# Local attention with a transposed product of values, and experts that start inside the attention stage before them

## The chip, the cores and the metric

The kernel runs on one core of one Trainium2 chip, in one launch. The metric is the time of an execution in microseconds (us). The core has four compute engines that run their own instruction streams side by side: TensorE (PE: matrix products and transposes), VectorE (DVE), ScalarE (ACT) and GpSimd (POOL). SyncE (SP) issues DMAs. Engines meet only through semaphores. PE writes into PSUM, which has eight banks, each of 512 fp32 numbers for each of 128 partitions; the other data lie in SBUF.

## The reference

A residual stream x of 2048 rows of 128 numbers goes through eight blocks, each `x = x + block(...)`:

```
linear attention
FFN block: 2 layers of local attention and gated FFN
small attention, global and local
FFN block again
head attention: softmax over the 16 heads of a row
experts
full attention: blocks of 256 rows, 2 heads
experts
```

The change touches four of them. The **FFN block** works on 2 x 1024 rows, so on 16 tiles of 128 rows, twice (2 layers). Cut to what matters, one layer is

```
h = shift_token(x)                 # half of the channels come from the row before
q, k, v = split(h @ wqkv)          # 8 heads of 64
q, k = rotary(l2norm(q) * qs, l2norm(k) * ks)
sim = q @ k^T  over windows of 64 rows and the window before, masked
x = x + (softmax(sim) @ v) @ wo
h = layernorm(shift_token(x)) @ w1 + b1
x = x + (a * gelu(g)) @ w2 + b2    # a, g = the halves of h, 341 wide
```

The **experts** are

```
logits = x @ Ws.T + bs;  probs = softmax(logits)     # 8 experts
route = argmax(probs);   xf = x * max(probs)
perm = argsort(route)                                # rows sorted by expert
y = relu(xf[perm] @ W1[e] + b1[e]) @ W2[e] + b2[e]
out = row i of the result is y of the i-th routed row (in sorted order)
```

The sorted rows go back into the stream in their sorted places, so each row's place has to be known before its result can be sent.

## The kernel before, in words

Eight stages stand in one program: linear attention, `windows(0)`, `small_heads`, `windows(1)`, `head_attention`, `experts(0)`, `full_attention`, `experts(1)`. After each stage every engine drains and adds to `batch_done`; SP waits for all four, sets the semaphores back to zero (`clear`) and lets them go on through `batch_go`.

Nothing plans the order. Each engine has its own loop over steps t, and the order of calls in that loop's body is the order of its instructions.

**`windows(F)`** runs 32 tiles (16 tiles, 2 layers) as a pipeline. In step t PE computes the scores of tile t (L522: 32 products in two banks), projects q and k of tile t + 2 (L531, L534), turns q and k of tile t + 1 (`turn_qk`, L550 and L557), turns the normalised output of tile t - 2 (`turn_out`, L593), turns the probabilities of tile t - 1 (`turn_probs`, L568), multiplies the output of tile t - 2 by wo (`out_rows`, L600), multiplies the probabilities of tile t - 1 by v (`values`, L582) and projects v of tile t + 2 (L541). Four tiles make a group for the FFN: its products (L625 up, L637 down) and its transposes (L328) stand in fixed steps. A cycle of four steps therefore repeats eight times in a pass and sixteen times in the program. Its steps are called A (down, first gates), B (last gate, L328), C (first two values of the FFN, `g_hm`) and D (last value, L328 of the FFN's input). A step begins with L522.

DVE takes the masked scores with their row minima (L1677), rotates q and k (L1684, L1685), sums the squares (L1706, L1707), adds the attention's output to the rows (`add_out`, L1700), multiplies the FFN's halves (`mid`, L1721), takes the reciprocal of the softmax sums (L1712) and scales the product of values with it (`norm_out`, L1668). Statistics of a group's shifted rows are L1456 and L1463. ACT squares q and k (L1103, L1105), copies banks to SBUF (L980), takes the exponentials (L1136) and the gelu (L1171, L1172). POOL adds the halves of the rotated pairs (`turn_pairs`, L2222, L2225), takes a power for the norms of q and k (L2232, L2235) and multiplies k with its own (L2233). SP copies the rows before a window (`lookback`) and the shifted rows of the FFN's input (`shift`, L2414 and L2415), in this order in each step.

**`head_attention`** has 16 tiles. For each, POOL multiplies 2048 columns of probabilities by values (`mix`, L2279) and DVE forms and adds up products of the same size (L1836, L1863).

**`experts(k)`** has a front for each of four chunks of 512 rows: variance (L1971, L1974), centring (L1982), normalisation on ACT, transposes, logits, shift (L1987 and the two after it), softmax and argmax (`route`, L1996 to L2005), scaled transposes, ranks on PE, prefix sums (L2012, L2013). POOL fetches each row's bias with an indirect DMA of one row per partition (L2319, 16 of them). Then 32 units follow, one for each pair of chunk and expert: PE up (L903), ACT relu, PE down (L911), DVE adds the rows that belong to the expert (L2034). After unit 8 DVE computes all rows' places (L2019 to L2023, `e_idx`), and POOL sends the 16 tiles of finished rows, with an indirect DMA each (L2329). A send needs its places and its chunk's last unit. The sorted rows are read back by SP (L2397). The first unit waits for the four biases of chunk 0.

## Time and profile before

| | us |
|---|---|
| median of 3 runs | 1928.71 (1919.35 to 1932.64) |
| the profiled execution | 1929.18 |
| its span in the profile | 1927.4 |
| PE busy in the span | 1617.2 (84%) |
| DVE busy | 1223.1 (63%) |
| ACT busy | 1071.9 (56%) |
| POOL busy | 906.4 (47%) |
| mean granted clock of TensorE | 0.916 of full speed |

The stages show in the trace as follows, by the first and last instructions of each: linear attention to about 328 us, `windows(0)` to about 720, `small_heads` to about 1058, `windows(1)` to about 1450, head attention from 1451 to 1599, the first experts to 1699, full attention to 1827, the second experts to the end. A row of a timeline gives start and length in us, engine, line, operation, the buffers written and read, how many instructions were joined to one row, and in brackets how long the engine had been idle before and what ended it. The busy shares are means over stages with different limits, so a wait counts only in the stage in which it ends last.

### The profile page before, as it was taken

The numbers are of one execution on the slowest core, as the hardware profiler recorded it, in microseconds if no ns is written. First come the engines' busy times: TensorE is split into PE (matmuls) and PEld (weight loads), VectorE is DVE, ScalarE is ACT, GpSimd is POOL, SyncE is SP. The second block draws the span as 40 slices with busy tenths as digits, with TensorE's granted clock in tenths as the row PEclk, the third lists the DMA queues.
The fourth block names the chain that finished last, engine by engine and source line by source line (L and its number), as shares of the span: only waits on it lengthen the run. The fifth ranks groups of instructions, "written<-read, shape, count | busy, mean of one in ns | idle before, by whom it ended". The sixth has DMA issues, their size and how long they took to land.

```text
span 1927.4 us, 37986 instructions
## 1 busy us (share of the span) xinstructions
PE 1617.2 (84%) x13323; PEld 1156.0 (60%) x13323; DVE 1223.1 (63%) x3746; ACT 1071.9 (56%) x2753; POOL 906.4 (47%) x668
## 2 busy tenths in 40 slices
PE   5999997799999977899787799999976666958777
PEld 5999995566666643344454466666644544636555
DVE  3555554887777644555763787777746985636565
ACT  3655653788888834566542678888842113323332
POOL 1333333776667512223443777667614673422044
PEclk9999998999999987899776999999987896968989
DMA  5000000111111100000000111111100001210012
GB/s 208 1 2 1 1 2 6 26 34 26 33 27 29 25 5 1 1 1 2 1 2 1 25 32 27 29 31 27 33 6 0 1 1 39 23 28 1 15 30 23
DMA packets 41082, 38.64 MB, mean 20 GB/s; under 512 B 21944, under 2 KB 32192, under 8 KB 40512
## 3 DMA queue, kind: packets, MB, share of 16 engines
q1 hardware_dynamic: 35264, 32.02, 6.4%
q0 software_dynamic: 5632, 4.20, 1.8%
q8 instruction: 110, 1.80, 0.4%
q14 instruction: 76, 0.62, 0.1%
HBM read 13.14 MB, written 4.20 MB: 9 GB/s over the span
## 4 chain that ended last, share of the span: by engine, by line
PE 46%; DVE 15%; issue 11%; POOL 7%; ACT 4%; DMA 1%; POOLq 0%; DVEq 0%; SPq 0%; ACTq 0%
PE ps L687 4%; PE ps L625 3%; PE ps L522 3%; PE ps L531 3%; PE ps L328 3%; PE ps L568 3%; PE ps L582 2%; PE ps L534 2%; PE ps L600 2%; PE ps L903 2%; PE ps L637 2%; PE ps L700 2%; PE ps L541 2%; PE ps L911 2%; POOL arena L2279 1%
## 5 line engine op out<-in xcount | busy, mean ns | idle before, releaser
L980 ACT ACTIVATE arena<-ps 128x512 f32<-128x512 f32 (+4 forms) x670 | 356.8, 589 | 273.8 <-PE ps L328 100.1
L1219 ACT ACTIVATE arena<-ps 128x320 f32<-128x320 f32 (+4 forms) x256 | 132.5, 561 | 136.5 <-PE ps L687 133.6
L1136 ACT ACTIVATE arena<-arena,g_small 128x128 f32<-128x128 f32 x512 | 198.7, 406 | 0.5
L2182 POOL TENSOR_TENSOR arena<-arena,consts 128x512 f32<-128x512 f32 (+1 forms) x64 | 93.1, 1455 | 195.3 <-ACT arena L1219 195.2
L1677 DVE CUSTOM_DVE_ANT_0 arena<-ps,consts,g_ss 128x128 f32<-128x128 f32 x512 | 145.6, 347 | 58.7 <-PE ps L522 58.7
L2222 POOL TENSOR_TENSOR arena<-arena 128x512 f32<-128x512 f32 x64 | 81.9, 1279 | 176.8 <-DVE arena L1685 176.8
L687 PE MATMUL ps<-arena 32*128 32x160 f32 (+4 forms) x1024 | 123.0, 471 | 22.6 <-ACT arena L1219 10.2
L328 PE MATMUL ps<-consts,arena 128*128 128x128 f32 x400 | 80.9, 339 | 59.1 <-ACT arena L1332 11.8
L1684 DVE TENSOR_TENSOR arena<-ps,tabs 128x512 f32<-128x512 f32 x128 | 87.7, 686 | 52.7 <-ACT arena L1105 46.0
L687 PEld LDWEIGHTS ps<-arena 32*128 32x128 f32 x1024 | 62.1, 214 | 91.1 <-ACT arena L1219 54.1
L328 PEld LDWEIGHTS ps<-consts,arena 128*128 128x128 f32 x400 | 55.6, 172 | 98.0 <-DVE arena L1475 20.6
L2232 POOL TENSOR_TENSOR g_ss<-g_ss,consts 128x8 f32<-128x8 f32 x64 | 105.4, 1647 | 9.7 <-DVE g_ss L1707 3.7
L1559 DVE TENSOR_REDUCE arena<-arena 128x8 f32<-128x1032 f32 x32 | 39.3, 1228 | 109.3 <-ACT arena L1037 109.3
L2279 POOL TENSOR_TENSOR arena<-arena 128x2048 f32<-128x2048 f32 x16 | 86.9, 5442 | 44.6 <-ACT arena L1241 44.6
L625 PE MATMUL ps<-arena,weights 128*128 128x512 f32 (+1 forms) x192 | 96.0, 610 | 13.6 <-ACT arena L1165 5.6
L2153 POOL TENSOR_TENSOR arena<-arena,consts 128x8 f32<-128x8 f32 x32 | 52.7, 1648 | 113.6 <-DVE arena L1559 113.6
L1136 ACT ACTIVATION_READ_ACCUMULATOR arena<-arena,g_small 128x1 f32 x512 | 105.1, 205 | 0.0
L2235 POOL TENSOR_TENSOR g_ss<-g_ss,consts 128x8 f32<-128x8 f32 x64 | 104.8, 1638 | 0.0
L749 PE MATMUL ps<-arena,consts 128*128 128x256 f32 x256 | 72.4, 446 | 34.5 <-DVE arena L1836 34.5
L2034 DVE SCALAR_TENSOR_TENSOR arena<-ps,arena 128x128 f32<-128x128 f32 x256 | 72.0, 344 | 42.8 <-PE ps L911 30.3
L700 PE MATMUL ps<-arena 128*32 128x160 f32 (+4 forms) x1024 | 88.7, 420 | 5.0 <-issue 5.0
L522 PEld LDWEIGHTS ps<-arena 64*64 64x64 f32 x2048 | 57.6, 135 | 58.4 <-issue 58.4
(257 smaller groups left out, 4170.3 us busy)
## 6 DMA issues: line engine op xcount, KB each, us to landing
arena<-arena SPq DMA_DIRECT2D x112, 128.0 KB, 2.3
weights<-in_w SPq DMA_DIRECT2D x1, 5069.0 KB, 24.2
weights<-in_w SPq DMA_DIRECT2D x1, 2052.0 KB, 12.6
arena<-Y SPq DMA_DIRECT2D x64, 32.0 KB
arena<-Y SPq DMA_DIRECT2D x64, 31.8 KB
consts<-in_c SPq DMA_DIRECT2D x1, 1278.0 KB, 8.7
sorted_rows<-X SPq DMA_DIRECT2D x1, 1024.0 KB, 5.1
X<-sorted_rows SPq DMA_DIRECT2D x4, 256.0 KB, 3.5
```

What stands on the lines that cost most here:

```text
L328: last = tr(ps[:, bank, j * P:(j + 1) * P], src(j), ident)
L522: last = mm(ps[64 * r:64 * r + 64, 4 + hf, i * P:(i + 1) * P], g_qT[rows, i, 64 * r:64 * r + 64], g_kT[rows, i, at:at + P], start=True, st ...
L625: mm(ps[0:m, 4 + c % 2, :], W("f_w1", at, at + m), g_hnT, start=True, stop=True)\
L687: last = mm(ps[:, 2 * (st % 2) + hh, 0:n], b_kT[rows, k % 2, r, j * P:(j + 1) * P], b_qT[rows, k % 2, j * P:j * P + n], start=True, stop=True)
L700: last = mm(ps[rows, 6 + U % 2, j * P:j * P + n], b_vx[:, k % 2, j, g, :], b_p[:, U % 2, g, at:at + n], start=j == 0, stop=True, skip_grou ...
L980: copy = lambda o, i: act.activation(o, i, ACT.Copy)
L1136: last = act.activation(g_p[:, n % 2, 4 * hf + i, :], g_sc[:, 4 * hf + i, :], ACT.Exp, scale=-1.0, bias=g_mn[:, h:h + 1], accum_out=g_rs[: ...
L1219: act.activation(b_p[:, U % 2, 2 * gp:2 * gp + 2, at:at + n], ps[:, b:b + 2, 0:n], ACT.Exp, scale=float(HD) ** -0.5).then_inc(s.b_exp, 1)
L1677: last = dve.tensor_tensor_reduce(g_sc[:, 4 * hf + i, :], ps[:, 4 + hf, i * P:(i + 1) * P], C("mask_f" if n % NT else "mask_f0"), g_ss[:, ...
L2232: stepped_after(pool.tensor_tensor(ss[:, 8:16], ss[:, 8:16], C("neghalf", 0, 8), ALU.pow))
L2235: pool.tensor_tensor(ss[:, 0:8], ss[:, 0:8], C("neghalf", 0, 8), ALU.pow).then_inc(gs.root, 1)
L2279: pool.tensor_tensor(c_mix[:, u % 2].rearrange("p (h d t) -> p h d t", h=HB, t=HB), c_e[:, u % 2].unsqueeze(2).broadcast_to(full), vals.un ...
```

## The change

It has two parts.

In **`windows`** the product of values swaps its operands: v becomes the stationary side and the turned probabilities the moving one, so that the output comes out with heads and channels on partitions, as `out_rows` needs it. The number and size of the products stay. `turn_out` and `norm_out` are gone. Since a row's reciprocal can no longer be applied after the product, the probabilities are scaled ahead of `turn_probs`: the even heads by DVE (`scale_even`, at the end of the tile's own step), the odd ones by POOL (`scale_odd`, first in the step after). `turn_probs` waits for the scaled halves. ACT copies the output from bank 3 as the first thing of a step (`keep_out`), and `out_rows` moves ahead of `turn_probs`. On DVE the statistics of the FFN's input move one step earlier (from `at_step` 7 to 6), behind the minima; `add_out` goes between the rotations, the FFN's multiplications ahead of the sums of squares.

In the **experts** the drain, `clear` and `batch_go` ahead of both expert stages are gone. Their SBUF area moves behind that of the attention. The front of chunk 0, and the variances of the first chunks, stand in the last steps of the attention stage; those of chunks 1 to 3 stand at units 0, 7 and 14 and the six after each. DVE computes all places after unit 19. The first unit no longer adds to fetched biases, so it doesn't wait for their DMA; POOL adds them later. In the first experts the last tile's sums and the last addition of head attention stand between the units 3 and 7.

```diff
+        front_bank, up_banks, down_banks = (4, 7), ((0, 1), (5, 6)), ((2, 3), (0, 1))
+        turned_at = (None, 0, 7, 14)
...
-                    pe.wait_ge(gs.exp, 2 * N + hf + 1)
+                    pe.wait_ge(gs.odd if hf else gs.even, N + 1)
...
-                    need(pe, gs.os, N)
+                    need(pe, gs.oin, N)
                     need(pe, gs.hin, m0 + groups_by(t, -3))
                     need(pe, gs.y, m0 + groups_by(t, 12))
-                    for h in range(HF):
+                    for i in range(4):
                         for r in range(2):
-                            src = g_v if r else g_vx
-                            last = mm(ps[64 * r:64 * r + 64, 3, h * DF:(h + 1) * DF],
-                                      g_pT[:, 4 * (h % 2) + h // 2, 64 * r:64 * r + 64],
-                                      src[:, j, h * DF:(h + 1) * DF], start=True, stop=True, skip_group_check=True)
+                            for hf in range(2):
+                                h, src = 2 * i + hf, g_v if r else g_vx
+                                last = mm(ps[64 * hf:64 * hf + 64, 3, i * P + 64 * r:i * P + 64 * r + 64],
+                                          src[:, j, h * DF:(h + 1) * DF], g_pT[:, 4 * hf + i, 64 * r:64 * r + 64],
+                                          start=True, stop=True, skip_group_check=True)
                     last.then_inc(gs.pv, 1)
-
-                def turn_out(n):
-                    N = n0 + n
-                    pe.wait_ge(gs.os, N + 1)
-                    pe.wait_ge(gs.vin, n0 + tiles_by(n + 3))
-                    need(pe, gs.add, N)
-                    for c in range(4):
-                        last = tr(ps[:, 2, c * P:(c + 1) * P], g_os[:, c * P:(c + 1) * P], ident)
-                    last.then_inc(gs.ot, 1)
 
                 def out_rows(n):
                     N, l = n0 + n, n // 16
                     pe.wait_ge(gs.oin, N + 1)
+                    pe.wait_ge(gs.vin, n0 + tiles_by(n + 3))
+                    need(pe, gs.add, N)
                     for c in range(4):
                         last = mm(ps[:, 2, 0:D], g_oT[:, c, :], W("f_wo", 512 * l + 128 * c, 512 * l + 128 * c + 128),
                                   start=c == 0, stop=c == 3)
                     last.then_inc(gs.out, 1)
...
-                        turn_out(t - 2)
+                        out_rows(t - 2)
...
                 def keep_out(n):
                     N = n0 + n
-                    act.wait_ge(gs.ot, N + 1)
+                    act.wait_ge(gs.pv, N + 1)
                     need(act, gs.out, N)
-                    copy(g_oT, ps[:, 2, :].rearrange("p (c t) -> p c t", c=4)).then_inc(gs.oin, 1)
+                    copy(g_oT, ps[:, 3, :].rearrange("p (c t) -> p c t", c=4)).then_inc(gs.oin, 1)
...
+                    if live(t - 2):
+                        keep_out(t - 2)
                     if live(t + 2):
                         squares(t + 2)
                     if live(t + 1):
                         keep_qk(t + 1)
-                    if live(t - 2):
-                        keep_out(t - 2)
...
-
-                def norm_out(n):
+                halves = lambda t: t.rearrange("p (i f) -> p f i", f=2)
+
+                def reciprocals(n, hf):
                     N = n0 + n
-                    dve.wait_ge(gs.pv, N + 1)
-                    need(dve, gs.ot, N)
-                    tt(heads(g_os), heads(ps[:, 3, :]), wide(g_ri, [P, HF, DF], 2), ALU.mult).then_inc(gs.os, 1)
+                    ri, rs = halves(g_ri)[:, hf, :], halves(g_rs[:, n % 2, :])[:, hf, :]
+                    dve.wait_ge(gs.exp, 2 * N + hf + 1)
+                    if hf:
+                        need(dve, gs.odd, N)
+                        dve.reciprocal(ri, rs).then_inc(gs.odd_ri, 1)
+                    else:
+                        need(dve, gs.even, N)
+                        after(dve.reciprocal(ri, rs), True)
+
+                def scale_even(n):
+                    probs = g_p[:, n % 2, 0:4, :]
+                    tt(probs, probs, wide(halves(g_ri)[:, 0, :], [P, 4, P], 2), ALU.mult).then_inc(gs.even, 1)
...
-                    if at_step(t, 7):
+                    if live(t):
+                        minima(t, 0)
+                    if live(t - 1):
+                        reciprocals(t - 1, 1)
+                    if fresh:
+                        norm_var(0)
+                    if live(t):
+                        minima(t, 1)
+                    if at_step(t, 6):
                         dve.wait_ge(gs.sh, 176 * (m0 + group + 1))
                         norm_stats(1, g_h)
-                    if live(t):
-                        minima(t, 0)
-                    if fresh:
-                        norm_var(0)
-                    if at_step(t, 7):
                         norm_var(1)
-                    if live(t):
-                        minima(t, 1)
                     if live(t + 2):
                         rope_k(t + 2)
+                    if live(t - 2):
+                        add_out(t - 2)
                     if fresh:
                         norm_apply(0, y, x, gs.ln)
                     if live(t + 2):
                         rope_q(t + 2)
-                    if live(t - 2) and at_step(t, 10):
-                        add_out(t - 2)
-                    if live(t + 2):
-                        sums(t + 2)
-                    if live(t - 2) and not at_step(t, 10) and not at_step(t, 12):
-                        add_out(t - 2)
+                    for lag, half, c in FFN_STEPS:
+                        if half == 1 and at_step(t, lag):
+                            mid((t - lag) // 4, c)
                     if at_step(t, 7):
                         need(dve, gs.hnt, m0 + group)
                         norm_apply(1, g_hn, g_h, gs.h2)
-                    if live(t - 1):
-                        reciprocals(t - 1)
+                    if live(t + 2):
+                        sums(t + 2)
+                    if live(t):
+                        reciprocals(t, 0)
+                        scale_even(t)
                     if at_step(t, 12):
                         add_down((t - 12) // 4)
-                    if live(t - 2) and at_step(t, 12) and not at_step(t, 10):
-                        add_out(t - 2)
-                    for lag, half, c in FFN_STEPS:
-                        if half == 1 and at_step(t, lag):
-                            mid((t - lag) // 4, c)
-                    if live(t - 1):
-                        dve.wait_ge(gs.dve_step, stepped.n)
-                        norm_out(t - 1)
...
+                    if t == 12:
+                        shift_routed(0, 0)
...
+                    if t == 13:
+                        route(0, 0)
+                    if t == 15:
+                        prefix(0, 0)
                     z, r = (t + 6) // NT, (t + 6) % NT
                     if z < NB and r == 0:
...
-                        prefix(q // 3 + 1)
-                    if q == 8:
-                        places_of_all()
+                    if k == 0 and q == 3:
+                        values(TT - 1)
+                        centre(0, 2)
+                    if k == 0 and q == 7:
+                        add_rows(NB - 1)
+                        variance(0, 3)
+                    if q == (9 if k == 0 else 1):
+                        centre(k, 3)
+                    for c in range(1, NB):
+                        if q == turned_at[c]:
+                            shift_routed(k, c)
+                        elif q == turned_at[c] + 1:
+                            route(k, c)
+                        elif q == turned_at[c] + 5:
+                            prefix(k, c)
+                    if q == turned_at[3] + 5:
+                        places_of_all(k)
...
+                def scale_odd(n):
+                    probs = g_p[:, n % 2, 4:8, :]
+                    ri = g_ri.rearrange("p (i f) -> p f i", f=2)[:, 1, :]
+                    pool.wait_ge(gs.odd_ri, n0 + n + 1)
+                    pool.tensor_tensor(probs, probs, ri.unsqueeze(2).broadcast_to([P, 4, P]), ALU.mult)\
+                        .then_inc(gs.odd, 1)
...
                 for t in range(-4, TILES + 9):
+                    if live(t - 1):
+                        scale_odd(t - 1)
...
+                fetch_biases(0)
+                fetch_biases(1)
+                if k == 0:
+                    root_routed(0, 3)
+                fetch_biases(2)
+                pool.wait_ge(b2_sem[0], 16 * NT * (k + 1))
+                pool.wait_ge(es.e_acc_in, (E * NB - 1) * k + E)
+                pool.tensor_tensor(e_acc[:, 0:NT, :], e_acc[:, 0:NT, :], e_bias, ALU.add).then_inc(es.e_bias_in, 1)
+                fetch_biases(3)
                 pool.wait_ge(es.e_idx_in, k + 1)
                 pool.wait_ge(es.e_kept, 16 * (k + 1))
+                pool.wait_ge(es.e_bias_in, k + 1)
...
-                sp.wait_ge(batch_done, 4)
-                clear()
-            if STAGES >= 6:
+                sp.wait_ge(s.c_add, NB)
                 keep(scratch.rearrange("(i p) d -> p i d", p=P))
                 back()
-            if STAGES >= 7:
                 sp.wait_ge(batch_done, 1)
                 clear()
```

Three places show what moves. First PE in step C of `windows`; before:

```order
L522 MATMUL ps<-arena 64x128 x16
L531 MATMUL ps<-weights,arena 128x512
L534 MATMUL ps<-weights,arena 128x512
L550 MATMUL ps<-consts,arena 128x128 x4
L557 MATMUL ps<-consts,arena 128x128 x4
L593 MATMUL ps<-consts,arena 128x128 x4
L625 MATMUL ps<-arena,weights 128x512 x2
L568 MATMUL ps<-consts,arena 128x128 x8
L600 MATMUL ps<-weights,arena 128x128 x4
L582 MATMUL ps<-arena 64x64 x16
```

and with the change (L527 is L522, L599 is `out_rows`, L624 up, L573 `turn_probs`, L588 `values`):

```order
L527 MATMUL ps<-arena 64x128 x16
L536 MATMUL ps<-weights,arena 128x512
L539 MATMUL ps<-weights,arena 128x512
L555 MATMUL ps<-consts,arena 128x128 x4
L562 MATMUL ps<-consts,arena 128x128 x4
L599 MATMUL ps<-weights,arena 128x128 x4
L624 MATMUL ps<-arena,weights 128x512 x2
L573 MATMUL ps<-consts,arena 128x128 x8
L588 MATMUL ps<-arena 64x64 x16
```

The four transposes are gone, and `out_rows` no longer stands between `turn_probs` and `values`. Next DVE in the same step, behind the minima; before:

```order
L1684 TENSOR_TENSOR arena<-ps,tabs 128x512
L1685 TENSOR_TENSOR arena<-ps,tabs 128x512
L1684 TENSOR_TENSOR arena<-ps,tabs 128x512
L1685 TENSOR_TENSOR arena<-ps,tabs 128x512
L1700 TENSOR_TENSOR Y<-Y,ps 128x128
L1706 TENSOR_REDUCE g_ss<-arena 128x16
L1707 TENSOR_SCALAR g_ss<-g_ss 128x16
L1712 RECIPROCAL g_small<-g_small 128x8
L1721 SCALAR_TENSOR_TENSOR arena<-ps,weights,arena 128x512 x2
L1668 TENSOR_TENSOR arena<-ps,g_small 128x512
L1456 BN_STATS stats<-arena 128x6 x4
```

and with the change (L1476 to L1489 are the statistics, L1736 and L1737 the sums, L1694 the reciprocals, behind which `scale_even` follows):

```order
L1476 BN_STATS stats<-arena 128x6 x4
L1483 BN_AGGR mv<-stats 128x2 x4
L1489 TENSOR_SCALAR g_rstd<-mv 128x4
L1714 TENSOR_TENSOR arena<-ps,tabs 128x512
L1715 TENSOR_TENSOR arena<-ps,tabs 128x512
L1730 TENSOR_TENSOR Y<-Y,ps 128x128
L1714 TENSOR_TENSOR arena<-ps,tabs 128x512
L1715 TENSOR_TENSOR arena<-ps,tabs 128x512
L1745 SCALAR_TENSOR_TENSOR arena<-ps,weights,arena 128x512 x2
L1736 TENSOR_REDUCE g_ss<-arena 128x16
L1737 TENSOR_SCALAR g_ss<-g_ss 128x16
L1694 RECIPROCAL g_small<-g_small 128x4
```

The statistics, which wait for SP's shifted rows, and the FFN's multiplications now stand ahead of the sums. Last, DVE in the first experts with the change, around the places (L2085 is the unit's addition, four to a unit; L2067 writes `e_idx`):

```order
L2085 SCALAR_TENSOR_TENSOR arena<-ps,arena 128x128 x16
L2056 TENSOR_TENSOR arena<-arena,ps 128x8 x4
L2057 TENSOR_TENSOR arena<-ps,arena 128x32
L2063 TENSOR_TENSOR arena<-arena 128x1 x7
L2064 TENSOR_TENSOR arena<-arena 128x128
L2065 TENSOR_TENSOR arena<-arena 128x128
L2066 TENSOR_REDUCE arena<-arena 128x16
L2067 CAST e_idx<-arena 128x16
L2085 SCALAR_TENSOR_TENSOR arena<-ps,arena 128x128 x48
```

Behind `e_idx` 48 additions are left, which is 12 units; before there were 92, which is 23.

## Rows read from the trace of the kernel before

**Rows 1.** stretch: bounds, length, busy us per engine, TensorE clock, DMA share, GB/s.
```profile
1067.00:1403.00 336.00, 311.90 (x3252) 217.43 (x3252) 260.67 (x924) 270.71 (x801) 229.70 (x173) 0.98 0.13 29
```

**Rows 2.** timeline of TensorE, local attention: start, us, what, [idle before <-releaser].
```profile
500.41 1.10 PE L522 MATMUL ps<-arena 64*64 64x128 f32 x32 [0.16 <-DVE arena L1721]
...
522.91 1.10 PE L522 MATMUL ps<-arena 64*64 64x128 f32 x32
...
526.63 0.60 PE L593 MATMUL ps<-consts,arena 128*128 128x128 f32 x4
...
530.05 1.13 PE L600 MATMUL ps<-weights,arena 128*128 128x128 f32 x8
...
534.43 1.10 PE L522 MATMUL ps<-arena 64*64 64x128 f32 x32 [1.12 <-DVE arena L1721]
...
544.45 1.10 PE L522 MATMUL ps<-arena 64*64 64x128 f32 x32 [0.16 <-DVE arena L1721]
```

**Rows 3.** timeline of ScalarE, the same step.
```profile
526.94 0.61 ACT L1172 ACTIVATE arena<-arena 85x512 f32<-85x512 f32 x1
...
528.41 2.52 ACT L980 ACTIVATE arena<-ps 128x512 f32<-128x512 f32 x5
```

**Rows 4.** timeline of VectorE, the same step.
```profile
528.55 0.69 DVE L1684 TENSOR_TENSOR arena<-ps,tabs 128x512 f32<-128x512 f32 x1 [2.22 <-ACT arena L1105]
...
531.42 1.21 DVE L1706 TENSOR_REDUCE g_ss<-arena 128x16 f32<-128x1024 f32 x1
...
532.88 1.41 DVE L1721 SCALAR_TENSOR_TENSOR arena<-ps,weights,arena 128x512 f32<-128x512 f32 x2
...
534.80 0.86 DVE L1456 BATCH_NORM_STATS2 stats<-arena 128x6 f32<-128x128 f32 x4
...
536.69 0.38 DVE L1463 BATCH_NORM_AGGREGATE mv<-stats 128x2 f32<-128x6 f32 x4
```

**Rows 5.** timeline of GpSimd, the same step.
```profile
529.92 1.28 POOL L2222 TENSOR_TENSOR arena<-arena 128x512 f32<-128x512 f32 x1 [4.64 <-DVE arena L1685]
...
532.92 1.65 POOL L2232 TENSOR_TENSOR g_ss<-g_ss,consts 128x8 f32<-128x8 f32 x1 [0.37 <-DVE g_ss L1707]
534.65 1.04 POOL L2233 TENSOR_TENSOR arena<-arena,g_ss 128x512 f32<-128x512 f32 x1
```

**Rows 6.** timeline of SyncE's DMA queue, the same step.
```profile
526.58 0.92 SPq L2415 DMA_DIRECT2D arena<-Y  x1
```

**Rows 7.** timeline of VectorE, inside head attention.
```profile
1523.72 2.94 DVE L1883 SCALAR_TENSOR_TENSOR c_nm<-mv,g_rstd 128x4 f32<-128x4 f32 x1
```

**Rows 8.** timeline of GpSimd, the same moment.
```profile
1521.19 5.45 POOL L2279 TENSOR_TENSOR arena<-arena 128x2048 f32<-128x2048 f32 x1 [2.42 <-ACT arena L1241]
```

**Rows 9.** timeline of VectorE, end of head attention, then first experts.
```profile
1591.94 2.29 DVE L1863 TENSOR_REDUCE ps<-arena 128x128 f32<-128x2048 f32 x1 [2.08 <-POOL arena L2279]
...
1608.06 0.19 DVE L1987 TENSOR_TENSOR arena<-ps,rows 128x32 f32<-128x32 f32 x1 [4.03 <-PE ps L883]
...
1610.72 0.69 DVE L2005 TENSOR_TENSOR arena<-arena 128x512 f32<-128x512 f32 x1
...
1626.66 1.12 DVE L2034 SCALAR_TENSOR_TENSOR arena<-ps,arena 128x128 f32<-128x128 f32 x4 [5.78 <-DMA arena<-bias_rows,e_rt]
...
1649.14 0.17 DVE L2023 CAST e_idx<-arena 128x16 uint32<-128x16 f32 x1
...
1684.91 1.13 DVE L2034 SCALAR_TENSOR_TENSOR arena<-ps,arena 128x128 f32<-128x128 f32 x4 [0.62 <-PE ps L911]
```

**Rows 10.** timeline of GpSimd, last of the first experts' sends.
```profile
1694.10 1.56 POOL L2329 DMA_INDIRECT sorted_rows<-arena,e_idx  x1 [0.30 <-issue]
```

**Rows 11.** timeline of SyncE's DMA queue, end of the first experts.
```profile
1697.43 2.02 SPq L2397 DMA_DIRECT2D X<-sorted_rows  x4
```

**Rows 12.** timeline of VectorE, full attention's last rows, second experts' first unit.
```profile
1826.51 0.17 DVE L1932 RECIPROCAL m_rs<-m_rs 128x2 f32<-128x2 f32 x1 [2.16 <-PE ps L845]
...
1854.94 1.13 DVE L2034 SCALAR_TENSOR_TENSOR arena<-ps,arena 128x128 f32<-128x128 f32 x4 [5.83 <-DMA arena<-bias_rows,e_rt]
```

509 lines of the change are left out of this document (260 added, 249 removed).

## The prediction

> **What bounds the kernel now.** I read the stages first. In the second pass of local attention TensorE is busy in 311.9 of 336 us at nearly full clock, while VectorE and ScalarE stay near 80% [rows 1]. So that stage goes by TensorE, and a microsecond taken from TensorE is a microsecond gained, as long as nothing that TensorE waits for comes later. Next comes TensorE's timeline for one cycle [rows 2]. The scores of step A start at 500.41 and those of the next A at 544.45, so four tiles take 44.04; C, from 522.91 to 534.43, takes 11.52 of it. In the whole cycle TensorE waits visibly twice, 1.12 in front of D and 0.16 in front of A, both times for `mid`.
>
> The experts are bound otherwise. The last `mix` ends at 1591.91, where VectorE starts its last sum, and the first unit starts at 1626.66 after a wait for the fetched biases [rows 9]: 34.7 us with no unit. From there to the reading back at 1697.43 [rows 11] it is 70.8. VectorE's units stand 1.75 apart (1.13 busy, 0.62 idle in front, at 1684.91 [rows 9]), and the last four sends 1.86 apart (1.56 busy, 0.30 idle) [rows 10]. In the second experts the gap from the last rows of attention, 1826.51, to the first unit at 1854.94 is 28.4 [rows 12].
>
> **Local attention, what goes.** `turn_out` costs TensorE from 526.63 to the next product at 527.07, 0.44 us for each of 64 tiles: 28.2 us. The wait of 1.12 in front of D goes too, since `mid` now stands ahead of the sums, and the 0.16 in front of A: 1.3 in a cycle. The swapped products keep their count and size, and I cost them at nothing (bounds: 32 records in 1.1 us either way; the width that moves is 64 in both). `norm_out` leaves VectorE; `scale_even` comes, of the same size as a rotation's product at 0.69 [rows 4], so its load hardly changes.
>
> **Local attention, what comes.** Times are counted from the start of C (522.91).
>
> 1. ScalarE's second gelu ends at +4.6, since its table load and two gelus stand ahead of the step [rows 3]. `keep_out` takes 0.5 (five copies in 2.52), so `out_rows` can start at about +5.2. TensorE is ready for it at +3.7, where `turn_out` stood [rows 2]. Before, the copy stood there too, but the up products and `turn_probs` hid it. TensorE waits about 1.4.
> 2. `out_rows` (530.05, 1 us) stood between `turn_probs` and `values` and hid ScalarE's copy of the turned probabilities. In C nothing is left between the two; the copy and its two semaphores cost about 0.8. In A, B and D products of the FFN stand there.
> 3. SP's last shifted rows are issued at +3.7 to +4.6 [rows 6], behind `lookback`, and nothing in the change moves that. With some 1.6 for landing they are there at +6.2. VectorE now waits for them in C; before, it read them in D. Then statistics 0.86 and the two small steps, 1.4 together, four rotations 2.4, `add_out` 0.2, `mid` 1.3, sums 1.4 [rows 4]: the sums end at +12.9. Before they ended at +9.9.
> 4. GpSimd's power takes 1.65 and the product with k 1.04 [rows 5]: k is ready at about +15.6, which is +3.9 in D. TensorE wants it at +3.3, and waits about 0.7.
> 5. The second power, 1.64, and `scale_odd` follow. The nearest row for the latter is the product with k, 1.04, the same size with a broadcast factor; the other bound is `turn_pairs` at 1.28 [rows 5]. I take 1.04. The odd half of `turn_probs` waits about 0.8 in D. The delay is not made up in D, where VectorE has no idle time: A begins with 0.2 and 0.8 of the same two waits.
>
> A cycle: -1.76 - 1.3 + 1.4 + 0.8 + 0.7 + 0.8 + 1.0 = +1.6. Sixteen cycles give +26. At the ends of each pass, where TensorE has no other tiles, the scalings stand in the open: some 2 us a pass, +4. **Local attention: +30.** From +24 (each wait 0.1 less) to +38 (`scale_odd` at 1.28 in every tile on the path).
>
> **First experts.** The first unit no longer waits for a DMA and starts about when the last `mix` ends: -34.7. Put into the attention's last steps are two variances, 2.8 together, and a chunk's shift and route, from 1608.06 to the end of the scaling at 1611.4, 3.4 [rows 9]. Centring is a few hundred numbers, but in head attention such an instruction took 2.94 us: it began at 1523.72 and ended with a `mix` of 5.45 that began at 1521.19 [rows 7, 8]. Two of them: 5.9. Prefix and what route meets of a `mix`: about 2. So the attention is later by 14. The units: before, nine of them with two fronts and the places took 22.6, from 1626.66 to 1649.3. Now `e_idx` needs eleven more units (19.3), one front (3.4) and the last sums, addition and variance of head attention (2.6 + 0.7 + 1.4): 50.0. Then 15 sends at 1.86, 27.9, and from the last one to the reading back 3.3, with 0.4 to the first: 81.6 against 70.8, +10.8. GpSimd is the bound there: the last unit would be done at 50 + 12 x 1.75 = 71. Sum: -34.7 + 14 + 10.8 = **-10**.
>
> **Second experts.** -28.4, and about 6.7 for what is left between the last values and the first unit; three variances and a route in the attention, 7.6 (there is no `mix`); the unit stage is longer as above without head attention's sums, 6.1. **-8**. What the missing drains save lies in these gaps.
>
> **Sum.** 1929.2 + 30 - 18 = 1941.2 for the profiled execution, against a median of 1928.7 that is 0.5 lower. I predict **1941**, slightly slower. About 1%, or 19 us, is what can be told from no change: between 1909 and 1948 is the same.
>
> The Trainium skill ("SBUF — State Buffer", "Who interferes with whom") says that a VectorE instruction with two SBUF inputs and a GpSimd instruction that reads SBUF exclude each other, the later one blocking fully. The 2.94 us above agree. By that rule `scale_even`, whose two inputs lie in SBUF, would wait for `turn_pairs` or the powers, and the sum would be rival 2's.
>
> **Rivals.**
>
> 1. *The waits don't appear, and TensorE keeps its 28 us.* It needs the copy of the output, the sums and `scale_odd` in time. For it: TensorE's 93% [rows 1], and GpSimd idle for 4.64 before `turn_pairs` [rows 5], room for 1.04. Against it: the place behind the gelu and SP's rows, which are orders in the code. Time: 1929.2 - 28 - 18 = 1883. Chance 0.25.
> 2. *VectorE and GpSimd hold each other up in every tile* (slower). `scale_even` starts with GpSimd's power and is held for its 1.65; then the next minima are late, and a chain that had 20% to spare on VectorE loses 0.5 in each of 64 tiles: +32. Time: 1973. It decides if a `scale_even` takes over 1.5 us. For it: [rows 7, 8]. Against it: `mid`, with two inputs in SBUF, took its 0.7 each at 532.88 while the power ran from 532.92 [rows 4, 5]. Chance 0.15.
> 3. *The experts gain the whole gap.* If the parts in the attention fit into VectorE's waits for `mix` (2.08 us in the last step [rows 9]) and the sends are not the bound, each stage gains about 28, together -56: 1929.2 + 30 - 56 = 1903. Against it: sixteen sends after `e_idx`, a count in the code. Chance 0.13.
>
> The forecast has the remaining 0.47, from 1918 to 1962 by its own bounds (24 to 38 for local attention; -30 to -5 for the experts, if the centrings are not held or if route is held twice).
>
> Faster by over 1%: rival 1 nearly whole and half of 3, 0.31. Slower by over 1% (over 1948): rival 2 and a third of the forecast, 0.31. The same: 0.38. The range goes from 1880, which takes in most of rival 1, to 1966; outside are rival 2 and the best ends of 1 and 3 together.
>
> **What would show it.** Right: in step C TensorE waits for ScalarE's copy ahead of `out_rows` and ahead of `values`, VectorE waits for a DMA behind the minima, and in D the transposes of k and of the odd probabilities wait for GpSimd; a cycle of 45.5; `e_idx` at 50 us after the first unit, and 16 sends in a row. Wrong: a cycle of 42 to 43 (rival 1), `scale_even` longer than 1 us (rival 2), or sends that end with the last unit (rival 3).

## The result

| | before | changed |
|---|---|---|
| median | 1927.51 us (1919.35 to 1932.64, 4 runs) | 1961.22 us (1958.54 to 1964.84, 4 runs) |
| profiled execution, its span | 1929.18, 1927.4 | 1962.28, 1960.4 |

The changed kernel is slower by 1.5%: ratio 1.0152, 95% interval 1.0115 to 1.0189. The forecast was 1941 with a range of 1880 to 1966 and 0.31 for slower by over 1%. The time lies in the range; the likeliest case had its sign, and about a third of its size.

The table splits the difference of the two spans, 33.0 us, by stages. Each border is the start or end of an instruction that both traces show.

| stretch | before | changed | difference | forecast |
|---|---|---|---|---|
| to the first statistics of head attention | 1451.1 | 1492.4 | +41.3 | +30 |
| from there to the end of the last `mix` | 140.8 | 155.4 | +14.6 | +14 |
| to the first unit | 34.7 | 0 | -34.7 | -34.7 |
| first unit to the reading back | 70.8 | 84.1 | +13.3 | +10.8 |
| full attention, first statistics to last rows | 126.3 | 137.0 | +10.7 | +7.6 |
| to the first unit | 28.4 | 7.4 | -21.0 | -21.7 |
| first unit to the end | 72.5 | 81.4 | +8.9 | +6 |

(0.1 lies between the reading back and full attention.) The second half of the change gains 8.2 in all; the first loses 41.3. Of these, 35.9 lie between the first and the last scores of the two passes of local attention. Some stages also differ between traces of the same instructions: from the last scores of the first pass to the first of the second it is 403.7 before and 406.4 changed, but 400.4 in the trace of `e_only` and 415.6 in that of `e_centre` below, which have the same code there; the granted clock between 720 and 1058 us was 0.83 and 0.77. A difference of a few microseconds in that stretch or in head attention is therefore no reading of the change.

**Local attention.** TensorE's waits from 350 to 650 us, total, times and longest. Before, the first was the one for `mid`:

```profile
PE ps L522 <- DVE arena L1721: 6.3, 10, 1.1
```

With the change they are:

```profile
PE ps L588 <- ACT arena L996: 13.6, 17, 1.4
PE ps L573 <- POOL arena L2285: 9.8, 13, 1.7
PE ps L599 <- ACT arena L996: 6.6, 5, 1.4
PE ps L562 <- POOL arena L2265: 5.4, 8, 1.3
```

These are `values` (L588) and `out_rows` (L599) behind ScalarE's copies, and the odd half of `turn_probs` (L573) and the transposes of k (L562) behind GpSimd's multiplications. TensorE was busy in 284.1 of these 300 us before and is in 259.4 now. Its timeline, with the same columns and for the same tiles as in [rows 2]; 535.07 begins the step C that began at 522.91 there:

```profile
532.68 1.15 PE L588 MATMUL ps<-arena 128*64 128x64 f32 x32 [0.71 <-ACT arena L996]
...
535.07 1.10 PE L527 MATMUL ps<-arena 64*64 64x128 f32 x32 [0.18 <-issue]
...
540.26 1.16 PE L599 MATMUL ps<-weights,arena 128*128 128x128 f32 x8 [1.30 <-ACT arena L996]
...
542.98 1.04 PE L573 MATMUL ps<-consts,arena 128*128 128x128 f32 x8
544.75 1.15 PE L588 MATMUL ps<-arena 128*64 128x64 f32 x32 [0.74 <-ACT arena L996]
...
547.27 1.10 PE L527 MATMUL ps<-arena 64*64 64x128 f32 x32 [0.32 <-DVE arena L1745]
...
551.37 0.66 PE L562 MATMUL ps<-consts,arena 128*128 128x128 f32 x4 [0.64 <-POOL arena L2265]
...
553.97 0.66 PE L573 MATMUL ps<-consts,arena 128*128 128x128 f32 x4 [0.62 <-POOL arena L2285]
...
558.00 1.10 PE L527 MATMUL ps<-arena 64*64 64x128 f32 x32
```

TensorE waits 1.30 for the copy ahead of `out_rows`, 0.74 ahead of `values`, 0.32 for `mid` at D's start, 0.64 for k and 0.62 for the odd half in D. B, whose end is the first row, waits 0.71 ahead of `values`; that one the forecast didn't have. ScalarE, VectorE, GpSimd in that order, each with the timeline's columns:

```profile
539.12 0.61 ACT L1188 ACTIVATE arena<-arena 85x512 f32<-85x512 f32 x1
539.64 0.57 ACT L996 ACTIVATE arena<-ps 128x512 f32<-128x512 f32 x1
```

```profile
541.73 0.87 DVE L1476 BATCH_NORM_STATS2 stats<-arena 128x6 f32<-128x128 f32 x4 [3.17 <-DMA arena<-Y]
...
547.05 1.21 DVE L1736 TENSOR_REDUCE g_ss<-arena 128x16 f32<-128x1024 f32 x1
...
548.58 0.71 DVE L1698 TENSOR_TENSOR arena<-arena,g_small 128x512 f32<-128x512 f32 x1
```

```profile
548.54 1.65 POOL L2264 TENSOR_TENSOR g_ss<-g_ss,consts 128x8 f32<-128x8 f32 x1 [1.32 <-DVE g_ss L1737]
550.27 1.05 POOL L2265 TENSOR_TENSOR arena<-arena,g_ss 128x512 f32<-128x512 f32 x1
551.27 1.64 POOL L2267 TENSOR_TENSOR g_ss<-g_ss,consts 128x8 f32<-128x8 f32 x1
552.87 1.05 POOL L2285 TENSOR_TENSOR arena<-arena,g_small 128x512 f32<-128x512 f32 x1
```

`keep_out` stands behind the gelu at +4.6 (539.64), as [rows 3] let expect. VectorE waits 3.17 for SP's rows and begins the statistics at +6.7, half a microsecond later than taken: SP issued the last of them at +3.7 to +4.6 as forecast, and they came 2.05 behind that, not 1.6; the sums (with L1737 behind the row shown) end at +13.4, not at +9.9 as in [rows 4]. GpSimd's k is there at 551.3, `scale_odd` (L2285) ends at 553.9, and TensorE's two rows in D start 0.05 to 0.06 behind each. `scale_odd` took 1.05 and `scale_even` (548.58) 0.71: both as taken.

The steps of the settled part of a pass (tiles 12 to 28 of its 32), start of the scores to start of the scores, for the kernel before and those that differ from it in local attention:

```
                 A      B      C      D     cycle
before         12.71   9.79  11.53  10.02   44.05
changed        13.32  10.06  12.20  10.73   46.31
w_only         13.32  10.06  12.20  10.72   46.30
w_no_odd       12.49  10.05  12.21  10.07   44.82
w_ko           13.32  10.05  12.20  10.72   46.29
w_ko_stats7    13.33  10.05  10.62  11.34   45.34
w_v_first      13.12  10.06  12.20  10.71   46.09
w_best         11.93  10.06  11.70  10.99   44.68
b_one_turn     12.72   9.78  11.52  10.02   44.04
b_eight_turns  13.00  10.09  11.53  10.03   44.65
```

**Experts.** VectorE at the end of head attention and in the first units, and GpSimd's sends with the `mix` that ran beside the first row:

```profile
1582.00 2.78 DVE L2023 SCALAR_TENSOR_TENSOR arena<-arena 128x4 f32<-128x4 f32 x1
...
1617.04 2.53 DVE L2039 TENSOR_TENSOR arena<-arena 128x32 f32<-128x32 f32 x1
...
1647.68 1.11 DVE L2082 TENSOR_SCALAR arena<-ps,arena 128x128 f32<-128x128 f32 x4
...
1699.78 0.17 DVE L2067 CAST e_idx<-arena 128x16 uint32<-128x16 f32 x1
```

```profile
1579.35 5.42 POOL L2320 TENSOR_TENSOR arena<-arena 128x2048 f32<-128x2048 f32 x1 [2.42 <-ACT arena L1257]
...
1700.23 1.63 POOL L2375 DMA_INDIRECT sorted_rows<-arena,e_idx  x1 [4.78 <-DVE e_idx L2067]
...
1728.37 1.57 POOL L2375 DMA_INDIRECT sorted_rows<-arena,e_idx  x1 [0.31 <-issue]
```

The centring of chunk 0 (L2023) took 2.78 and ended at 1584.78, as the `mix` did (1584.77): the instruction was held, as [rows 7, 8] showed of its like. That of chunk 1 fell between two `mix` and took 0.15. A product of `route` (L2039) was held for 2.53. The first unit (L2082) starts 0.05 before the last `mix` ends, in place of 34.7 behind it [rows 9]. `e_idx` comes 52.1 behind the first unit, and then the sixteen sends stand in a row to 1728.37, the reading back following at 1731.78.

In full attention the last rows begin at 1871.67 and the first unit at 1879.05, where [rows 12] had 28.4 between the two:

```profile
1871.67 0.17 DVE L1968 RECIPROCAL m_rs<-m_rs 128x2 f32<-128x2 f32 x1 [2.16 <-PE ps L856]
...
1879.05 1.13 DVE L2082 TENSOR_SCALAR arena<-ps,arena 128x128 f32<-128x128 f32 x4 [3.88 <-PE ps L938]
```

The stage is longer by 10.7 where 7.6 was forecast. TensorE's queue shows one reason: the scaled transposes of chunk 0 stand ahead of the last products of attention and wait for VectorE's `route`:

```profile
1861.54 1.12 PE L333 MATMUL ps<-consts,arena 128*128 128x128 f32 x4 [3.18 <-DVE arena L2046]
```

### The profile page after: what moved, and what is told of

Read it like the earlier page. It is cut to its first block and busy times, and to the rows that moved or that the text cites. A ratio compares the mean times of both kernels' runs of the same rounds, so it can differ in the third digit from the quotient of the medians.

```text
span 1960.4 us, 37569 instructions
## 1 busy us (share of the span) xinstructions
PE 1597.3 (81%) x13067; PEld 1126.3 (57%) x13067; DVE 1242.6 (63%) x3810; ACT 1078.4 (55%) x2753; POOL 978.9 (50%) x734
## 5 line engine op out<-in xcount | busy, mean ns | idle before, releaser
L996 ACT ACTIVATE arena<-ps 128x512 f32<-128x512 f32 (+4 forms) x670 | 371.0, 578 | 345.5 <-PE ps L333 92.8
L333 PE MATMUL ps<-consts,arena 128*128 128x128 f32 x400 | 76.5, 325 | 44.5 <-DVE arena L1672 10.5
L624 PE MATMUL ps<-arena,weights 128*128 128x512 f32 (+1 forms) x192 | 98.7, 624 | 14.0 <-ACT arena L1181 7.5
L746 PE MATMUL ps<-arena,consts 128*128 128x256 f32 x256 | 77.1, 468 | 34.8 <-DVE arena L1855 34.8
L588 PEld LDWEIGHTS ps<-arena 128*64 128x64 f32 x2048 | 65.6, 138 | 65.9 <-ACT arena L996 33.3
L588 PE MATMUL ps<-arena 128*64 128x64 f32 x2048 | 74.1, 225 | 29.0 <-ACT arena L996 29.0
L1152 ACT ACTIVATION_READ_ACCUMULATOR arena<-arena,g_small 128x1 f32 x512 | 97.4, 190 | 0.0
L599 PE MATMUL ps<-weights,arena 128*128 128x128 f32 x512 | 72.8, 287 | 27.9 <-ACT arena L996 27.9
```

Of the source, the lines that this page charges most:

```text
L333: last = tr(ps[:, bank, j * P:(j + 1) * P], src(j), ident)
L588: last = mm(ps[64 * hf:64 * hf + 64, 3, i * P + 64 * r:i * P + 64 * r + 64], src[:, j, h * DF:(h + 1) * DF], g_pT[:, 4 * hf + i, 64 * r:64 ...
L624: mm(ps[0:m, 4 + c % 2, :], W("f_w1", at, at + m), g_hnT, start=True, stop=True)\
L996: copy = lambda o, i: act.activation(o, i, ACT.Copy)
L1152: last = act.activation(g_p[:, n % 2, 4 * hf + i, :], g_sc[:, 4 * hf + i, :], ACT.Exp, scale=-1.0, bias=g_mn[:, h:h + 1], accum_out=g_rs[: ...
```

## The experiments

**The two halves apart.** `w_only` is the kernel before with the change in `windows` and nothing else, `e_only` the reverse; the edit is the diff ahead of the prediction, cut in two.

> The kernel before with the change in local attention alone; head attention and experts are as before. My theory (the two parts add up, and local attention carries the loss): head attention starts 41 us later in the trace of the changed kernel, and everything behind it is as before, so 1928 + 41 = 1969, with the same cycle of 46.3. The rival (part of those 41 us comes from the other half of the change, by its memory layout or its code) expects under 1960.

> The kernel before with the change in the experts alone. My theory, from the two traces: the first experts gain 34.7, lose 14.6 in the attention before them and 13.3 in their units and sends; the second gain 21.0 and lose 10.7 and 8.9; together -8, so 1920. The rival (the missing drains are worth more, and the late start of both stages in the changed kernel hides it) expects 1900 or less.

Measured: w_only 1973.8 us, ratio to before 1.0217 (1.0169 to 1.0265); e_only 1918.5, ratio 0.9966 (0.9934 to 0.9997). The rivals fall: local attention alone loses some 42 us with the same steps, and the experts alone gain 0.3%, 6.5 us by that ratio (12.5 by the medians), with the 8 expected inside the interval. Within these intervals the halves add up.

**GpSimd's multiplication left out.**

```diff
-                    pool.tensor_tensor(probs, probs, ri.unsqueeze(2).broadcast_to([P, 4, P]), ALU.mult)\
-                        .then_inc(gs.odd, 1)
+                    pool.sem_inc(gs.odd, 1)
```

> As w_only, without GpSimd's multiplication of the odd heads' probabilities: they stay unscaled, the semaphore is raised all the same. My theory (GpSimd's chain of powers, product with k and this product ends TensorE's waits in A and D, and part of B): the waits of turn_probs go, the ones for k go partly, the cycle falls from 46.3 by 1.3 to 1.6, that is 21 to 26 us less than w_only. Rival 1 (VectorE's late sums set the pace, GpSimd's product only stands in their shadow): under 8 us less. Rival 2 (the shared SBUF port): over 35 less, since the products of both engines no longer meet.

Measured: 1945.1 us, ratio 1.008 (1.0033 to 1.0126), 29 less than w_only. The cycle fell by 1.48, inside the expected 1.3 to 1.6; A lost 0.83 and D 0.65. Rival 1 is out (under 8), and so is rival 2 (over 35). One multiplication of 1.04 us in each tile costs 24 us in the sixteen cycles, 0.37 a tile, though GpSimd was idle for a quarter of this stage (busy 226.6 of 300 us in w_only): in two of the four steps it stands last in a chain, in the other two (10.05 and 12.20 with it, 10.05 and 12.21 without) it costs nothing.

**Which waits are worth what.** Four kernels change the order of w_only.

```diff
 # w_ko, ScalarE's loop
-                    if live(t - 2):
-                        keep_out(t - 2)
...
+                    if live(t - 1):
+                        keep_out(t - 1)
                     if at_step(t, 9):
                         gelu((t - 9) // 4)
 # w_ko_stats7, besides: VectorE
+                    if at_step(t, 7):
+                        dve.wait_ge(gs.sh, 176 * (m0 + group + 1))
+                        norm_stats(1, g_h)
                     if live(t):
                         minima(t, 0)
 # w_v_first, on w_only, TensorE
-                    if live(t - 1):
-                        values(t - 1, t)
                     if live(t + 2):
                         project_v(t + 2, t)
+                    if live(t - 1):
+                        values(t - 1, t)
```

`w_best` is w_ko_stats7 with w_v_first's order and the sums ahead of `mid`.

> As w_only, with two orders changed: ScalarE copies the output of a tile at the end of the step, ahead of the gelu, instead of behind it at the start of the next; and VectorE's statistics of the shifted rows go back to step D, ahead of the minima. My theory (the place behind the gelu and the wait for SP's rows are two of the four losses): TensorE's 1.3 in C ahead of out_rows and VectorE's 3.2 are gone, the waits for GpSimd in D shrink; the cycle falls to between 44.5 and 45.2, that is 18 to 29 us less than w_only. The rival (one wait takes the other's place) expects within 6 us of w_only.

> As w_only, with ScalarE's copy of the output at the end of a step, ahead of the gelu; the statistics stay in step C, behind the wait for SP's rows. Theory 1 (the waits add up): the 1.3 us ahead of out_rows in C are saved in each cycle, 20 us less than w_only. Theory 2 (the chain from SP's rows through VectorE's sums and GpSimd sets when k of step D is ready, so TensorE reaches D earlier and waits there): C falls by 1.3 or more, D grows by nearly as much, at most 6 us less than w_only. I hold theory 2 for likelier, 0.7.

> As w_only, with the projection of v for tile t + 2 ahead of the product of values of tile t - 1 on TensorE, so that 1 us of work stands where TensorE waited for ScalarE's copy of the turned probabilities. Theory 1 (that wait is lost time in B and C): 0.7 in each of two steps, cycle 46.3 to 44.9, 22 us less than w_only. Theory 2 (in C the chain from SP's rows sets the end of the step, only B can gain): cycle to 45.6, 8 to 12 us less. Theory 3 (B's gain too is only waited for later, at GpSimd's half of turn_probs): under 4 us less. I hold theory 2 for likeliest.

> As w_ko_stats7, with the sums of squares ahead of the FFN's multiplications on VectorE, as before the change, and the projection of v ahead of values on TensorE: every order that was found to cost is undone or filled, and the four transposes stay away. Theory 1 (the transposes filled a gap in which TensorE would have waited for ScalarE's copies of q and k, so leaving them out saves nothing, and GpSimd's multiplication of the odd heads still costs): cycle 44.2 to 45.0, 1935 to 1945, no faster than before. Theory 2 (TensorE's 28 us come out once the new waits are gone): cycle under 43.2, 1915 or less.

Measured, as ratios to before: w_ko_stats7 1.0113 (1.0057 to 1.0168), w_ko 1.0178 (1.0148 to 1.0208), w_v_first 1.022 (1.0182 to 1.0258), w_best 1.0035 (1.0008 to 1.0062), its median 1937.0.

In w_ko the wait of 1.3 is gone and no step is shorter. TensorE's table shows it again in front of D, for `mid` (L1716), up to 1.5:

```profile
PE ps L521 <- DVE arena L1716: 7.4, 5, 1.5
```

So theory 2 holds: C ends when the chain from SP's rows ends. Only with the statistics back in D does C fall, by 1.58, and D gives back 0.62; A stays. The cycle was 45.34, just outside the expected 44.5 to 45.2. In w_v_first the waits of `values` fell from w_only's 13.6 to 1.1 in the same 300 us, and the cycle by 0.2: theory 3, the one held for least likely. In its place TensorE waits at a step's start for ScalarE's copy of a gate (L1156), and the rows for GpSimd stay:

```profile
PE ps L567 <- POOL arena L2243: 10.7, 15, 1.7
...
PE ps L521 <- ACT arena L1156: 5.6, 5, 1.2
...
PE ps L582 <- ACT arena L971: 1.1, 2, 0.6
```

w_best came out as its theory 1 had it, 44.68 and 1937: without the four transposes, a cycle is still longer than with them. But the steps differ. A, in which TensorE has no idle row, is 0.78 shorter than before. The others end with longer waits: 1.16 ahead of C for the copy of a gate, 1.83 and 1.45 ahead of D and A for `mid`. In the same 300 us, where before it was 6.3 for `mid` and none for the gate, these are:

```profile
PE ps L521 <- DVE arena L1716: 16.4, 10, 1.8
...
PE ps L521 <- ACT arena L1156: 5.6, 5, 1.2
```

TensorE was busy in 261.6 of the 300 us, against 284.1 before. So its work is gone, and outside A the time was waited away. w_best still has `scale_odd`, and `mid` behind the sums. No run left `scale_odd` out of it or of w_ko_stats7, so what the new order of TensorE is worth without GpSimd in the chain is open.

**What the transposes were worth.** In the kernel before, three of a tile's four transposes are left out (b_one_turn), or all are done twice (b_eight_turns).

```diff
-                    for c in range(4):
+                    for c in range(1):                      # b_one_turn
+                    for c in (0, 1, 2, 3, 0, 1, 2, 3):      # b_eight_turns
                         last = tr(ps[:, 2, c * P:(c + 1) * P], g_os[:, c * P:(c + 1) * P], ident)
```

> The kernel before, with one transpose of a tile's output in place of four (the other three quarters of the output are left out), everything else the same. It asks what the removed TensorE work was worth by itself. Three transposes are 0.33 us in each of 64 tiles, 21 us. My theory (the stage goes by TensorE): 15 to 21 us less than before; the 1.3 us a cycle that TensorE waits for mid may take up to 6 of it back. The rival (TensorE's work was never the bound, the chain through GpSimd was) expects under 6 us.

> The kernel before, with a tile's four transposes of the output done twice, 0.43 us more of TensorE in each of 64 tiles, the same result. With three of four left out, the cycle of 44.04 stayed. Theory 1 (the four transposes just fill the gap in which turn_probs waits for ScalarE's copies of q and k, so work beyond them counts): A and B grow by 0.4 each, C and D by less, as they waited 1.1 and 0.2 for mid; cycle 45.0 to 45.8, 15 to 28 us slower. Theory 2 (the gap is wider, or TensorE is not what sets the step): cycle under 44.3, under 4 us slower.

b_one_turn: 1927.3 us, ratio 0.9978 (0.9951 to 1.0006), no step changed by over 0.01. The lower end of the interval alone would leave 9 us, the steps leave none. My theory falls. TensorE's timeline of its step A:

```profile
502.19 1.10 PE L522 MATMUL ps<-arena 64*64 64x128 f32 x32 [0.16 <-DVE arena L1721]
...
505.92 0.27 PE L593 MATMUL ps<-consts,arena 128*128 128x128 f32 x1
506.43 1.12 PE L568 MATMUL ps<-consts,arena 128*128 128x128 f32 x8 [0.24 <-issue]
```

In A the scores start at 502.19 and `turn_probs` at 506.43, 4.24 later, as before (500.41 and 504.65); the transpose is shorter, and an idle time of 0.24 stands behind it. From 350 to 650 us such idle times are 7.8 in 27 tiles, against 0.3 in one tile before, and the wait for `mid` is 6.3 in both:

```profile
PE ps L568 <- issue: 7.8, 27, 0.6
```

27 times the 0.33 that was left out is 8.9: nearly all of it came back as waiting. The profile names no releaser for it. By the code the first half of `turn_probs` waits for ScalarE's copy of the turned q, whose bank it overwrites. ScalarE's timeline of the kernel before has that copy as the first of the five behind the squares of k:

```profile
503.46 0.60 ACT L1105 ACTIVATE arena<-ps 128x512 f32<-128x512 f32 x1 [0.26 <-PE ps L534]
503.95 2.55 ACT L980 ACTIVATE arena<-ps 128x512 f32<-128x512 f32 x5
```

and in b_one_turn

```profile
505.74 2.55 ACT L980 ACTIVATE arena<-ps 128x512 f32<-128x512 f32 x5
```

`turn_probs` starts 0.70 and 0.69 behind these, and in C of the kernel before 0.69 behind 528.41 [rows 3]. Taken singly, the copy lasts 0.59 and `turn_probs` starts 0.10 behind its end in each step between 450 and 590 us of both kernels, whatever TensorE did just before. In b_eight_turns, where the transposes reach further, it starts in A, B and D 0.46 behind the copy and 0.11 behind the start of the last transpose, the usual distance between two transposes. So `turn_out` was work put into a gap. No run moved the copy; that it ends the gap is read from the code and from this constant distance, while the worth of the transposes in that order is measured. b_eight_turns: 1939.5, ratio 1.007 (1.0038 to 1.0101), cycle 44.65, between the ranges of both theories. A and B grew by 0.3 each, C and D by nothing, though each of them got 0.43 more. The gap in A and B ends about 0.1 behind the four transposes; in C and D TensorE has at least 0.43 to spare.

**The experts.** `e_early` brings the fronts closer, `e_centre` moves the centrings, `e_early_centre` does both and moves the variances as well.

```diff
-        turned_at = (None, 0, 7, 14)     # fronts; scaled transposes at + 5, ranks at + 6
+        turned_at = (None, 0, 5, 11)     # e_early; + 3 and + 4
 # e_centre, VectorE in head attention
                     if 0 <= t - 1 < TT:
                         shift(t - 1)
+                    if t in (9, 13):
+                        centre(0, t // NT - 2)
...
                     if t in (8, 12):
                         variance(0, t // NT - 2)
-                    if t in (9, 13):
-                        centre(0, t // NT - 2)
```

> As e_only, with the fronts of chunks 1 to 3 closer together: they begin at units 0, 5 and 11 instead of 0, 7 and 14, and a chunk's scaled transposes and ranks follow 3 and 4 units behind its start instead of 5 and 6. All places are then known after unit 14 instead of 19. Theory 1 (the sixteen sends behind the places bound the stage): from the first unit to the reading back it falls from 84 us to 79, where the last unit and its four sends (10.8) take over; 5 us in each stage, 1909. Theory 2 (TensorE and VectorE pace the units, the sends keep pace): nothing, 1918.

> As e_early, with the variances and centrings of chunks 0 and 1 ahead of the sum over the mixed values in head attention's steps, where GpSimd's mix of 5.4 us does not run, instead of at the end of the step, where it does. In the changed kernel they took 1.71, 2.78 and 1.06 there in place of 0.17. Theory (these small instructions are held by the shared read port until the mix ends, and VectorE's products wait behind them): each takes under 0.3, and head attention is 4 to 5 us shorter; 1905. The rival (mix is the bound, VectorE has the time): the instructions are short but the stage ends as before.

> As e_only, with the two centrings of head attention alone moved ahead of the sum over the mixed values; the variances stay at the step's end. Theory (a small instruction of VectorE with two SBUF inputs is held until GpSimd's mix ends): the centring of chunk 0 takes 0.15 in place of 2.91, and head attention from its first statistics to the end of the last mix falls by 2 to 3 us from 159.2; 1916 in place of 1918.5. The rival (VectorE has that time to spare) expects the same length.

e_early: ratio 0.9953 (0.9935 to 0.9971), median 1919.5. `e_idx` came 47.4 behind the first unit in place of 50.4, but the stage took 83.5 in place of 82.3 in e_only: twelve sends ran in a row, and then GpSimd waited for the last units:

```profile
1682.32 1.56 POOL L2376 DMA_INDIRECT sorted_rows<-arena,e_idx  x1 [4.49 <-DVE arena L2095]
```

Theory 2 is right: sends and units were nearly level, and the fronts put closer together slow the units.

e_early_centre: ratio 0.9977 (0.9957 to 0.9998). The centrings took 0.15 as expected. The variances' last instruction, one addition to 4 numbers in each partition, took 4.75, as it now fell behind the start of a `mix` at 1524.87:

```profile
1525.57 4.75 DVE L2027 TENSOR_SCALAR arena<-arena 128x4 f32<-128x4 f32 x1
```

Head attention took 160.7 in place of 159.2. e_centre leaves that one where it was (1.69, as in e_only 1.68):

```profile
1544.21 1.69 DVE L2027 TENSOR_SCALAR arena<-arena 128x4 f32<-128x4 f32 x1
...
1548.79 0.15 DVE L2033 SCALAR_TENSOR_TENSOR arena<-arena 128x4 f32<-128x4 f32 x1
```

The centring took 0.15 in place of 2.91. Head attention took 152.5 in this trace, but it had taken 155.4 in the changed kernel and 159.2 in e_only with the same instructions there, so that stage differs by more than the expected 2 to 3 from trace to trace. The granted clock in it was 0.85, 0.82 and 0.81 in these three; with the old order it was 0.84 before (140.8) and 0.87 in w_ko_stats7 (137.0). A rival is therefore that the 152.5 is the clock's. The ratio, 0.9932 (0.9904 to 0.9959), overlaps e_only's. That the instruction is held is shown; what its release is worth is not. The three other kernels with the change in the experts alone are also below the kernel before, by 0.2 to 0.5%; e_centre has the largest gain, 0.4 to 1.0%.

## Why the prediction came out as it did

1. *"A microsecond taken from TensorE is a microsecond gained"*, and `turn_out` as -28.2: wrong. This is the step that failed. b_one_turn took three quarters of that work away and gained nothing. The busy share of 93% [rows 1] was read as a bound; by the times, TensorE was that full because work had been laid into the gaps of a chain that runs TensorE, ScalarE, TensorE. The change itself moves `out_rows` into that gap, which b_one_turn doesn't test: there TensorE's work fell by about as much as forecast (busy 259.4 of 300 us in place of 284.1), and the waits grew by more. Local attention lost 41.3, above its own bounds of 24 to 38; the total stayed inside the range because that is wide.
2. *C*: forecast +0.64, measured +0.67, from the waits that were named (1.30 of 1.4, 0.74 of 0.8), and the wait for `mid` partly stayed (0.32 in D). TensorE's account closes: it waits 2.36 in place of 1.12 and works 0.56 less (0.44 forecast). But the account doesn't say what ends the step. w_ko shows that the wait ahead of `out_rows` alone decided nothing; the chain from SP's rows did, and a wait was added where a later one ends the step. That the sum was near is in part luck.
3. *B*: forecast -0.44, measured +0.27. "In A, B and D products of the FFN stand there": in B these are four transposes and one product, 1.3 us, and they don't cover the copies. TensorE waited 0.71 there.
4. *D and A*: forecast +0.90 (0.7 + 0.8 - 0.44 - 0.16) and +0.56, measured +0.71 and +0.61. Mechanism as named: k and the odd half from GpSimd, late because the sums were (+13.4; forecast +12.9). w_no_odd prices `scale_odd` at 1.48 a cycle. The size has luck in it: "+3.9 in D" takes C as 11.7 long, while the forecast's own terms make it 12.16, by which k would be there at +3.4 and the wait be 0.1. The half microsecond by which SP's rows came later made up for that.
5. *The cycle*: +1.6 forecast, +2.26 measured, 10.6 us over sixteen. The rest up to head attention, passes' starts and ends, was +4 and is about +5, which is within what the stage between the passes differs by from trace to trace.
6. *Experts*: first -10, measured -6.8; second -8, measured -1.4. The gaps were right. Head attention came to +14.6 for 14, but with other terms: one centring was held and not two (2.78 and 0.15, for 5.9), while the variances' last additions (1.71, 1.06 and 1.70 for 0.17) and a product of `route` (2.53 for 0.19) were held too; and in e_only the same stage was 18.4 longer than before. Mis-sized were the units (13.3 for 10.8, 8.9 for 6: VectorE waits 11.0 us for TensorE's down products between the first unit and `e_idx`, which came at 52.1 for 50.0) and full attention (10.7 for 7.6, where TensorE waits 3.18 behind `route`).
7. *Rival 1* (TensorE keeps its 28 us) had 0.25. It fell: the cycle was 46.31 and not 42 to 43, and in the order before most of these 28 us weren't there to be had. *Rival 2* (both engines hold each other up in every tile) fell too: 60 of the 64 `scale_even` took 0.69 to 0.72. The other 4 took 1.50 to 1.52, and its mechanism is in them, at too few places to count. The argument set against it, `mid` beside the power, was weak: the first of `mid`'s inputs is a bank of PSUM and the second a column of one number per partition. *Rival 3* fell too, yet its argument against, that sixteen sends bound the stage, is only half true: e_early.
8. *The bounds*: 1929.2 + 24 - 30 is 1923; the forecast's "from 1918" is a slip that decides nothing.

The Trainium skill's rule on the shared port ("SBUF — State Buffer", "Who interferes with whom") fits the held centrings, and the held `tensor_scalar`, the variances' additions, by its sentence on 2-port modes, which this kind of instruction can enter and in which it contends with GpSimd too. It fits the four long `scale_even` as well, which all began behind the start of GpSimd's product with k, VectorE first and then GpSimd:

```profile
358.30 1.51 DVE L1698 TENSOR_TENSOR arena<-arena,g_small 128x512 f32<-128x512 f32 x1
```

```profile
358.22 1.04 POOL L2265 TENSOR_TENSOR arena<-arena,g_ss 128x512 f32<-128x512 f32 x1
```

By the same page GpSimd's powers, which read SBUF, should hold `scale_even` too; they didn't: 54 of the 64 began while a power ran and took 0.69 to 0.72, as did the one at 548.58 beside the power of 548.54.

## What to carry to other kernels

A busy share near 100% tells that an engine is full, not that its work sets the time: before removing work, take a part of it out, and double it, and see which steps move. Do it in the order that the change will have, too: here the order before had the work in a gap, and the new order filled the gap with something else. Of waits in one step only the last counts, so price a new wait against the chain that ends the step and not as a sum. A short instruction on an engine with time to spare (here 1.04 us, the engine busy for three quarters of the stage) isn't free when it stands last in a chain between engines: it cost 0.83 and 0.65 in two of the four steps, and nothing where another chain was later.

## What the runs showed of the hardware

A VectorE addition to 128x4 numbers with one SBUF input, issued 0.7 us behind the start of a GpSimd product of 128x2048, took 4.75 us and ended with that product (`e_early_centre`), while statistics over 128x128 beside such a product kept their length (0.81 for four at 1572.87, changed kernel). The same addition took 0.17 with GpSimd idle (1671.52, changed kernel).

A VectorE product of 128x512 with two inputs in SBUF (`scale_even`) took 1.50 to 1.52 us in the 4 of 64 tiles in which it began 0.07 to 0.09 behind the start of a GpSimd product of 128x512. Beside a GpSimd power of 128x8, 1.65 us long, it took 0.69 to 0.72 in all 54 tiles in which it began within one.
